# Side operations of the middle iterations of a four-block kernel moved to another set of places in the instruction order

## The reference, cut to what matters

```
x = x + gate0 * unpermute(mamba(permute(norm(x) * scale0 + shift0)))   # block 0
x = x + film(softmax_attention(norm(x)))                               # block 1, 16 heads of 16
x = x + gate1 * mamba(norm(x) * scale1 + shift1)                       # block 2
x = x + film(linear_attention(norm(x)))                                # block 3

mamba: xm, z = split(h @ W_in)            # 512 channels each
       u = silu(causal_conv4(xm));  dt, B, C = f(u @ W_xp)
       h[t] = h[t-1] * exp(dt[t] * A) + dt[t] * u[t] * B[t]   # 512 channels x 16 states
       y[t] = sum over states of h[t] * C[t] + u[t] * D;  out = (y * silu(z)) @ W_out
```

## Time and profile before

| | us |
|---|---|
| median of three runs (lowest, highest) | 5416.12 (5393.92, 5426.02) |
| profiled execution | 5402.86 |
| its span, first to last instruction | 5401.1 |
| DVE busy in the span | 4656.6 (86%) |
| PE busy | 4461.0 (83%) |
| POOL busy | 4060.0 (75%) |
| ACT busy | 3281.6 (61%) |

### The profile page before, as it was taken

One profiled execution on the slowest core, in us unless ns is written; L12 is line 12 of the kernel. 1 busy time (PEld: TensorE's weight loads), 2 busy tenths in 40 slices (PEclk: granted clock), 3 DMA queues, 4 the chain that ended last, 5 costly groups with the idle time before them and its releaser, 6 DMA issues.

```text
span 5401.1 us, 54840 instructions
## 1 busy us (share of the span) xinstructions
PE 4461.0 (83%) x16792; PEld 2437.3 (45%) x16792; DVE 4656.6 (86%) x4552; ACT 3281.6 (61%) x5574; POOL 4060.0 (75%) x2840
## 2 busy tenths in 40 slices
PE   3678888888888888888888888888888888888765
PEld 1244444444444544444454444445444444544433
DVE  2885898999989898999998899898999999997573
ACT  2564565666666666766666676666666666665352
POOL 1874787878878787887877788777778878786562
PEclk8788798999989999999998999999999999998777
DMA  4763666666766676776666677666666766665362
GB/s 148 240 217 128 206 236 210 231 226 236 252 212 232 217 235 224 243 247 215 234 216 219 226 244 245 221 225 220 223 228 230 251 217 233 222 237 182 121 210 69
DMA packets 355050, 1164.53 MB, mean 216 GB/s; under 512 B 39347, under 2 KB 79330, under 8 KB 354758
## 3 DMA queue, kind: packets, MB, share of 16 engines
q1 hardware_dynamic: 310598, 1106.42, 59.9%
q10 hardware_dynamic: 44160, 54.60, 3.3%
HBM read 1140.78 MB, written 20.10 MB: 215 GB/s over the span
## 4 chain that ended last, share of the span: by engine, by line
DVE 34%; PE 31%; issue 11%; DMA 9%; ACT 8%; POOL 7%; SPq 1%; ACTq 0%; DVEq 0%; POOLq 0%
DVE hw L1234 16%; DVE ps L1220 7%; PE ps L1121 6%; PE ps L1472 5%; PE ps L1499 4%; DMA bs<-bc_scratch 4%; POOL hw L1252 4%; PE ps L893 3%; PE ps L1334 3%; ACT pts L1567 3%; DVE mx L1592 2%; DMA cs<-bc_scratch 2%; ACT da L1170 2%; DMA xhat<-in_x 2%; PE ps L1515 2%
## 5 line engine op out<-in xcount | busy, mean ns | idle before, releaser
L1252 POOL TENSOR_TENSOR hw<-hw,cs 128x1024 f32<-128x1024 f32 x1024 | 2416.0, 2359 | 755.4 <-DVE hw L1234 639.8
L1234 DVE TENSOR_TENSOR_SCAN hw<-da,ps 128x1024 f32<-128x1024 f32 x1024 | 2334.2, 2280 | 36.5 <-PE ps L1121 14.9
L1170 ACT ACTIVATE da<-dt,a_neg 128x510 f32<-128x510 f32 x2048 | 1327.0, 711 | 266.3 <-DVE hw L1234 262.8
L1259 POOL TENSOR_TENSOR hw<-hw 128x512 f32<-128x512 f32 x1024 | 1299.4, 1269 | 69.5
L1220 DVE TENSOR_TENSOR ps<-ps,bs 128x1024 f32<-128x1024 f32 x1024 | 1256.5, 1227 | 99.0 <-DMA bs<-bc_scratch 55.5
L1121 PE MATMUL ps<-hw,ident 128*128 128x512 f32 x2048 | 1135.1, 664 | 127.5 <-POOL hw L1259 127.3
L1121 PEld LDWEIGHTS ps<-hw,ident 128*128 128x128 f32 x2048 | 405.3, 211 | 593.5 <-issue 325.5
L893 PE MATMUL ps<-hT,w_in 128*128 128x512 f32 x1024 | 544.2, 663 | 83.9 <-DVE dt L1081 63.2
L1567 ACT ACTIVATE pts<-ps 128x512 f32<-128x512 f32 x512 | 280.2, 593 | 400.5 <-PE ps L1499 400.5
L1592 DVE TENSOR_REDUCE mx<-ps 128x2 f32<-128x512 f32 x512 | 330.0, 683 | 166.0 <-PE ps L1472 165.7
L770 ACT ACT_TABLE_LOAD x321 | 411.8, 1283 | 28.7 <-DVE x_c L1782 23.3
(11 more groups left out here) (180 smaller groups left out, 5370.7 us busy)
## 6 DMA issues: line engine op xcount, KB each, us to landing
bs<-bc_scratch SPq DMA_DIRECT2D x1024, 512.0 KB, 4.7
cs<-bc_scratch SPq DMA_DIRECT2D x1024, 512.0 KB, 4.8
taps<-taps_scratch SPq DMA_DIRECT2D x32, 512.0 KB, 6.7
xhat<-in_x ACTq DMA_DIRECT2D x16, 512.0 KB, 6.3
gate<-gates_scratch ACTq DMA_DIRECT2D x64, 128.0 KB, 4.9
x_b<-in_x ACTq DMA_DIRECT2D x16, 512.0 KB, 9.0
x_scratch<-x_b ACTq DMA_DIRECT2D x16, 512.0 KB, 5.8
x_c<-x_scratch ACTq DMA_DIRECT2D x16, 512.0 KB, 5.9
```

The source lines that it names most:

```text
L1170: ins = nc.scalar.activation(da[q % (AHEAD + 1)][:, k, :, 1:S], dt_[:, c, :].rearrange("p (b s) -> p b s", b=GB)[:, :, 1:S], ACT.Exp, scal ...
L1234: nc.vector.tensor_tensor_scan(tile[:, :, :].rearrange("p n t -> p (n t)"), da[s % (AHEAD + 1)][:, :, :, :].rearrange("p n b s -> p (n b s)"),
L1252: nc.gpsimd.tensor_tensor(tile[:, :, :], tile[:, :, :], cs[s % C_RING][:, :, :], ALU.mult)\
L1259: nc.gpsimd.tensor_tensor(tile[:, 0, :], tile[:, 0, :], tile[:, 1, :], ALU.add)\
```

## The change

All numbers of the tables "even" and "odd" in `PLACES` are replaced, for all pieces and the five engines. Nothing else is touched: the operations, their shapes, their waits and the tables "first", "second", "last_but_one", "last" and "end" are the same. The core of the diff, for the pieces and engines that the prediction speaks of:

```
     "even": {
         "attn_b": {
-            "pe": [-33.333, 1.7, 2.1, 3.033, 3.5, 3.7, 3.9, 4.1, 5.425, 5.675, 5.8, 6.05, 6.8, 8.55, 8.675,
+            "pe": [0.967, 1.6, 1.9, 2.2, 3.467, 3.633, 3.8, 4.133, 4.7, 5.1, 5.633, 6.8, 7.633, 7.8, 7.967,
...
-            "dve": [-67.333, -34.667, 5.553, 5.777, 6.11, 6.22, 6.464, 6.598, 6.732, 6.866, 7.165, 7.498, 7.665,
-                   7.832, 8.553, 8.777, 9.055, 9.11, 9.165, 9.275, 17.066, 17.132, 17.198, 17.264, 19.464,
-                   19.598],
-            "pool": [-100.5, 16.717, 16.883],
+            "dve": [-1.5, -0.5, 4.665, 5.165, 5.553, 5.777, 6.165, 6.665, 7.11, 7.22, 7.553, 7.777, 8.165,
+                   8.498, 8.665, 8.832, 9.498, 9.665, 9.832, 10.665, 17.464, 17.598, 17.732, 17.866, 19.665,
+                   20.082],
+            "pool": [0.275, 18.217, 18.383],
...
         "front1": {
-            "dve": [19.732, 19.866, 23.665, 25.665, 26.553, 26.777, 27.165, 27.553, 27.777],
+            "dve": [20.165, 20.247, 24.665, 25.165, 25.665, 27.665, 28.165, 28.665, 29.11],
...
         "mid1": {
-            "pe": [27.443, 27.586, 27.729, 27.871, 28.014, 28.157],
-            "act": [26.975, 28.5, 28.7, 28.9],
-            "dve": [30.165, 31.165],
+            "pe": [29.55, 29.675, 29.8, 29.925, 30.05, 30.175],
+            "act": [28.5, 28.7, 28.9, 29.6],
+            "dve": [30.665, 30.832],
...
         "rest0": {
-            "pe": [-66.667, 2.767, 5.55, 5.925, 6.175, 8.425, 9.05, 9.175],
+            "pe": [0.633, 3.967, 4.5, 4.9, 5.967, 7.467, 8.133, 10.767],
...
     "odd": {
         "attn_a": {
-            "dve": [5.832, 5.916, 11.027, 11.055, 11.082, 11.11, 11.165, 11.248, 11.275, 11.303, 11.397, 11.464,
-                   11.531, 11.598, 11.665, 11.732, 11.799, 11.866, 11.933, 12.11, 18.066, 18.132, 18.198,
-                   18.264, 20.665, 22.066],
+            "dve": [5.832, 5.916, 10.553, 10.777, 11.165, 11.442, 11.553, 11.665, 11.888, 12.041, 12.082,
+                   12.206, 12.248, 12.498, 12.665, 12.832, 13.082, 13.165, 13.248, 13.665, 19.055, 19.11,
+                   19.165, 19.275, 21.165, 21.665],
...
         "front0": {
-            "pe": [23.633, 23.967, 24.8, 25.54, 25.78, 26.02, 27.7, 27.9, 29.175],
-            "act": [20.3, 22.6, 23.65, 23.8, 23.95, 25.267, 25.433, 27.5, 27.7, 27.9, 29.85],
+            "pe": [24.633, 24.967, 25.471, 25.643, 25.814, 26.157, 26.9, 27.586, 30.8],
+            "act": [20.433, 23.65, 23.8, 23.95, 25.433, 26.433, 27.243, 27.386, 27.529, 27.957, 28.3],
...
         "mid0": {
-            "pe": [28.425, 28.55, 28.675, 28.8, 28.925, 29.05],
+            "pe": [27.729, 27.871, 28.014, 28.157, 28.633, 28.967],
```

More of the change, by code:

```diff
@@ L293 @@
+            "pool": [0.275, 18.217, 18.383],
+            "sp": [-0.364, -0.273],
         },
         "back1": {
[L295 to L299, removed]
+            "pe": [11.967, 14.05, 15.7],
+            "act": [10.6, 13.6],
+            "dve": [13.665, 14.165, 15.665, 16.11, 16.22],
+            "pool": [16.217, 16.383],
@@ L300 @@
+            "sp": [-0.727, -0.636],
         },
         "front1": {
-            "pe": [20.467, 20.633, 20.967, 21.133, 21.8, 25.9, 26.2, 26.82, 31.8],
-            "act": [18.6, 19.5, 19.7, 19.9, 20.767, 20.933, 25.6, 26.35, 26.475, 26.85, 28.3],
-            "dve": [19.732, 19.866, 23.665, 25.665, 26.553, 26.777, 27.165, 27.553, 27.777],
-            "pool": [19.3, 32.05],
-            "sp": [-0.022, 0.089],
+            "pe": [19.633, 19.967, 21.55, 21.8, 22.05, 22.633, 25.9, 26.9, 31.8],
+            "act": [19.767, 20.35, 20.6, 20.85, 21.35, 23.62, 23.86, 27.243, 27.386, 27.957, 28.3],
@@ L307 @@
+            "dve": [20.165, 20.247, 24.665, 25.165, 25.665, 27.665, 28.165, 28.665, 29.11],
+            "pool": [20.8, 32.05],
+            "sp": [-0.182, -0.091],
         },
         "lin_a": {
[L309 to L312, removed]
@@ L313 @@
-            "pool": [16.3, 26.3, 26.8],
-            "sp": [-0.467, -0.356],
+            "pe": [17.6, 17.9, 19.1, 22.967, 24.633, 24.967, 25.6, 26.2, 27.8, 28.8, 29.425],
+            "act": [16.671, 16.957, 17.35, 21.6, 21.85, 22.6, 23.74, 23.98, 24.6, 27.529, 27.671, 27.814],
+            "dve": [16.665, 17.165, 19.165, 20.665, 21.165, 21.665, 22.665, 23.165, 23.665, 24.165, 26.165,
+                   26.665, 27.165, 29.22, 30.497],
+            "pool": [17.3, 27.217, 27.383],
+            "sp": [-0.545, -0.455],
@@ L323 @@
         "rest0": {
-            "pe": [-66.667, 2.767, 5.55, 5.925, 6.175, 8.425, 9.05, 9.175],
[L325 to L328, removed]
+            "pe": [0.633, 3.967, 4.5, 4.9, 5.967, 7.467, 8.133, 10.767],
+            "act": [-1.5, 2.3, 4.6, 4.767, 4.933, 7.8, 8.267, 8.767, 8.933],
+            "dve": [3.165, 9.165, 11.165, 13.165],
+            "pool": [3.3, 9.3, 11.3, 11.8],
+            "sp": [-0.909, -0.818],
         },
@@ L344 @@
+            "pool": [6.3, 19.3, 19.8],
+            "sp": [-0.364, -0.273],
         },
         "back0": {
-            "pe": [2.1, 2.9, 3.633, 3.967, 4.8],
-            "act": [0.6, 4.6, 5.433, 5.767],
+            "pe": [2.1, 3.467, 3.633, 3.8, 3.967],
+            "act": [1.767, 3.433, 3.767, 6.3],
             "dve": [5.414, 5.498, 5.581, 5.665, 5.749],
-            "pool": [1.3, 2.8],
-            "sp": [-0.467, -0.356],
+            "pool": [4.717, 4.883],
+            "sp": [-0.545, -0.455],
@@ L358 @@
+            "dve": [22.497, 22.665, 26.665, 27.165, 28.22, 29.082, 29.165, 29.247, 31.83],
+            "pool": [23.3, 30.3],
+            "sp": [-0.182, -0.091],
         },
         "lin_b": {
[L360 to L363, removed]
@@ L364 @@
-            "pool": [11.8, 25.3, 26.8],
-            "sp": [-0.689, -0.578],
+            "pe": [12.9, 13.9, 15.586, 21.05, 22.55, 22.8, 23.05, 23.8, 25.986, 26.329, 27.443],
+            "act": [12.5, 12.7, 12.9, 15.9, 16.6, 18.6, 20.767, 21.433, 21.767, 25.767, 26.767, 27.671],
+            "dve": [12.165, 12.289, 14.665, 16.165, 16.665, 17.165, 17.665, 18.665, 19.22, 20.165, 22.832,
+                   23.165, 23.665, 28.11, 30.665],
+            "pool": [12.925, 24.8, 25.8],
+            "sp": [-0.727, -0.636],
@@ L366 @@
         },
         "mid0": {
-            "pe": [28.425, 28.55, 28.675, 28.8, 28.925, 29.05],
-            "act": [27.3, 28.6, 29.35, 29.6],
+            "pe": [27.729, 27.871, 28.014, 28.157, 28.633, 28.967],
+            "act": [27.814, 28.5, 28.7, 28.9],
             "dve": [31.11, 31.22],
@@ L374 @@
         "rest1": {
[L375 to L379, removed]
+            "pe": [-1.5, -0.5, 0.15, 1.7, 4.133, 7.8, 10.02, 12.7],
+            "act": [-1.667, -1.333, 0.033, 0.067, 1.433, 7.7, 8.433, 10.6, 12.3],
+            "dve": [-0.5, 9.665, 11.777, 12.124],
+            "pool": [3.3, 9.8, 12.675, 12.8],
+            "sp": [-0.909, -0.818],
         },
```

18 lines of the change are left out of this document (6 added, 12 removed), and 10 rows, old and new, of the table PLACES.

## The result

The change made the kernel 1.2% faster: 5348.92 us median of 4 runs (5339.05 to 5360.27) against 5419.95 us of 4 runs of before; ratio 0.9879, 95% interval 0.9841 to 0.9917. On two other chips it measured 0.9897 (0.9872 to 0.9921) and 0.9895 (0.9859 to 0.9931). The forecast was 5430, no change. The value lies in its range, 11 us under the rival *faster* (5360) and 12 under the short reckoning (5361).

The account below looks back on a forecast made before the run. DVE, busiest engine, was taken as the bound, idle 350.8 us in the 28 iterations. Even +0.5, odd -1.5 and scatter +2 made +1.0 a pair, +14 us for 14 pairs: 5430 us, range 5345 to 5530.

Parts of the forecast that it names:

- rival *faster: Spreading the odd maxima gains 4 us or more a pair if reduction 26 is done before scan 30: 5360; chance 0.26.
- short reckoning: Following the lists with 0.6 us for each side operation of DVE; without scatter the lower bound, -55 us.
- The choice of the odd iteration's value: Odd iteration: -2.6 us as followed without other effects, bounds -3.9 and +1.3; -1.5 was taken, near their middle.
- Scatter: Every iteration: 1 us added (0 to 1.5), since a followed path has fixed durations; +2 for a pair.
- The even iteration: Maxima and border of the even iteration together: +0.5 us, from 0 in the short to +2.4 in the long reckoning.
- The maxima: Even iteration, first maximum moved one step earlier, before product 5: -0.7 us, between -2.7 and +1.4.
- The border: End of the even iteration, `xp` behind reduction 27 and `dt0` before product 31: +1.2 us, between -0.3 and +3.1.
- long reckoning: Following the lists with the whole 0.7 us for each side operation of DVE; with scatter the upper bound, +94 us.
- Clearly slower: Late first scores in the even iteration and a longer PE end chain: 5479 (0.27), or a pile-up, 5556 (0.13); 0.40 in all.
- Clock: PE's granted clock falling to 0.90 as a rule would cost 69 us; counted within the slower case.
- L1599: Sign in odd iterations: DVE's wait at the additions behind the maxima falls from 2.0 us to nearly nothing.
- the maxima in the odd iteration: Sign: DVE's wait of the maxima for the scores falls from 7.2 us to under 2.

Follow-up runs that it names:

- e15: Changed kernel with the four `xp` of the odd iteration behind reduction 26 instead of ahead of it; ratio 0.9955 to the kernel before.
- e3: Changed kernel with all of POOL's lists as they were before; ratio 1.0196 to the kernel before.
- e4: Kernel before with POOL's places moved in two pieces, attn_b of the even and rest1 of the odd iteration; ratio 1.0136 to the kernel before.
- e7: Changed kernel with the odd table's pieces up to step 24 as before, on all engines; ratio 1.0347 to the kernel before.
- e8: Changed kernel with attn_b, rest0 and back1 of the even table as before; ratio 1.0228 to the kernel before.
- e9: Kernel before with the new odd table alone, on the second chip; ratio 0.9991 to the kernel before.
- e17: Changed kernel, even iteration: three last `cv` a half step earlier, an `xp` group a step earlier, `xo` ahead of product 29; ratio 0.9919 to the kernel before.

## Why the prediction was wrong

The sum of the parts is mis-sized in three terms, and the steps below it mostly stood.

1. **The choice of the odd iteration's value** ("I take -1.5, near their middle"). The list followed step by step gave -2.6: 7 us gained at the maxima, 4.4 given back. Measured: -2.7. Steps 5 to 12 gain 7.4, steps 0 to 4 and 13 to 29 give back 5.2, the last two gain 0.6. I had the number and moved away from it, towards a bound, for no row. 1.2 us in 14 iterations: 17 us. (The old list has eight maxima ahead of scan 11 and eight behind it, not ten and six; no term hangs on that.)
2. **Scatter** ("I add 1 us for an iteration"). Before has the same scatter: its even iterations run from 150.0 to 157.9, after's from 148.2 to 156.3, in the profiles shown first. A sum made as a difference against means of before must not carry it a second time: 28 us.
3. **The even iteration**, +0.5 forecast, -1.6 measured: 29 us. Its stated bounds, 0 to +2.4, are narrower than those of its own two parts (-2.7 to +1.4 and -0.3 to +3.1), and only the latter hold the value. The maxima gave 1.3 in place of 0.7. The border (steps 25 to 31), forecast at +1.2, came to -0.3: the wait of up to 0.8 for `out` did not come, and the longer waits for `dt` (1.97 and 1.37, forecast 1.0 to 1.4 and 0.9 to 1.2) took up most of that for the slice. Steps 11 to 20 gained 0.6 that stood in no term. Missed the other way was `krec`, which stands a step earlier than ACT has `kT` ready: +0.7.

17, 28 and 29 are the 74 us between the forecast's +14 and the measured -60 of the 28 iterations (the means above; -62 in the first profile).

**Short or long.** The long reckoning, a full 0.7 us for each side operation, was wrong in sign. DVE's busy time fell by 26 us over the 28 iterations, 43% of the gain, in all three profiles of after (4017.7, 4016.6, 4018.2 against 4043.6 and 4043.1), with the same instructions. A small operation alone between product and scan adds 0.47 to 0.52 us, one more beside it 0.59, where the long reckoning had 0.7 for each. So an order that sets small operations singly between large ones saves busy time as well as waits; that all of the 26 us come from this is not shown. The prediction took the larger figure as an equal possibility.

**The rivals.** *Faster* (0.26) is what happened, near its price (5360), by its mechanism as far as the odd iterations go (2.7 us of the 4.3 that a pair gained), but not on its condition: scan 30 does wait for reduction 26, 1.0 us where 1.9 was forecast, and the time fell all the same. e15 shows that the wait was the wrong test: with the order that avoids it other waits of 1.8 us stand in steps 30 and 31, and the kernel is 0.6% slower, in part perhaps by its clock. *Clearly slower*: of its two conditions the first did not come (0.9 us at the first maximum of the even iteration; it needed 3.5, and 2 was forecast), nor the second (scan 30 stands 1.0, not 4). *Clock*: in the 28 iterations 0.92 and 0.93 in the two profiles before, 0.93, 0.92 and 0.92 after; no part in the whole change. The experiments are another matter, as said there.

**The signs.** Right: L1599, the odd iterations shorter by 1 to 4. Right in kind, off in size: the maxima in the odd iteration (7.2 in the mean before; after, 3.4, above the 2 forecast) and scan 30 (1.0 for nearly 2). Wrong: even iterations longer by 0 to 2, the even wait of about 2 at the first maximum. One wait that the prediction named as a sign against it did come up, small: scans waiting for decays, 0.9 us before and 14.5 after over the 28 iterations. The table load that "now stands on the chain from the last `cv` to `dt0`" does not. ACT in iteration 15 after:

```profile
2647.80 0.63 ACT L985 ACTIVATE u<-u 128x512 f32<-128x512 f32 x1 [1.52 <-DVE u L1073]
2648.45 1.28 ACT L770 ACT_TABLE_LOAD   x1
...
2649.75 1.33 ACT L1170 ACTIVATE da<-dt,a_neg 128x510 f32<-128x510 f32 x2
2653.39 0.59 ACT L1027 ACTIVATE xd<-ps 96x512 f32<-96x512 f32 x1 [2.31 <-PE ps L917]
```

It ends at 2649.73, as the `xp` begin, and `xd` waits 2.31 for them. The drain of some 1.38 us that the Trainium skill ("ScalarE: Activation LUTs", What ACT_TABLE_LOAD costs) adds to a switch does not show here either: 0.02 us lie on each side of the load.

## What to carry to other kernels

Where a path followed instruction by instruction gives a number, forecast that number, and let bounds widen only the range; moving towards a bound and adding scatter that the kernel before has as well cost 45 of 74 us here. A wait on the busiest engine is worth its time only if nothing behind it is late by nearly as much: four single waits of 1 to 2 us were taken away here, none made the kernel faster, and in each case other waits came up within ten steps. Such an order is also easy to break from within: one engine's column or a few places of it (e3, e4) and the early part of one table (e7, e8), put into the other kernel, cost 1.4 to 4.5% against it, while a whole table alone lost nothing. And where PE's granted clock differs between two sets of runs, as it did in the parts here (0.893 against 0.900), a difference of half a percent is not yet that of the order: look at the clock beside each time.

## What the runs showed of the hardware

A small operation of DVE (506 to 512 elements, 0.68 to 0.74 us by its row) adds 0.47 to 0.52 us between two that run over 1024 elements, and one more next to it 0.59. With one and the same list of instructions, an even iteration took 149.0 us at a granted clock of 0.95 and 162.5 at 0.88 (e9), though DVE, the busiest engine, worked 143.3 and 144.0 us in them. The transfer of a slice of B at the border is ready at a time of its own: when the chain ahead of it was 1.1 us earlier (e17), its mean wait grew from 0.05 to 0.92. Two sets of runs of one kernel agreed within 0.11%, but one stretch, iteration 1, differed by 7 us between two executions of the kernel before.
